# First attention layer and feed-forward layer in one block: the feed-forward layer's work is ordered behind single batches

## The reference, cut to what matters

```python
# first attention: one head, attention over the 128 columns (128x128 scores per batch)
x = x + layernorm(attn(layernorm(x)))
# feed-forward with ternary weights
def ternary_linear(x, w):                       # w_t: signs of w where |w| > 0.5 mean|w|, else 0
    rms = sqrt(sum(x * x)) / sqrt(d)
    return (x / (rms + 1e-8)) @ w_t.T
x = x + layernorm(ternary_linear(gelu(ternary_linear(layernorm(x), w_up)), w_down))   # 128 -> 512 -> 128
```

## Time and profile before

| | |
|---|---|
| time, median of 3 | 1156.36 us (1156.05 to 1159.06) |
| the profiled execution | 1163.83 us, span 1161.9 us |
| busy in the span: PE, DVE, ACT, POOL | 907.8, 597.1, 781.1, 360.5 us |
| first_attention | 0 to 90.2 us of the span |
| feed_forward | 90.7 to 191.2 us |
| all later blocks | 191.2 to 1161.9 us |

### The profile page before, as it was taken

The page is one execution under the profiler, slowest core; times in us unless marked ns, Lnnn a source line. Parts: engine busy times, 40 slices in busy tenths (PEclk is TensorE's granted clock), DMA queues, the critical chain, the costliest instruction groups (busy, mean ns, idle before and its releaser), DMA issues. The chain is left out here.

```text
span 1161.9 us, 19219 instructions
## 1 busy us (share of the span) xinstructions
PE 907.8 (78%) x6570; PEld 428.5 (37%) x6570; DVE 597.1 (51%) x2007; ACT 781.1 (67%) x1186; POOL 360.5 (31%) x332
## 2 busy tenths in 40 slices
PE   3754984765399999999989999998869878696650
PEld 3642763332021222222222222232357556365550
DVE  7387856888100444444443325342353236686557
ACT  1233342436499999999989999995565665675530
POOL 6312433445300000000000000222576477766743
PEclk8676986887699999999999999998959999898885
DMA  3000001235751212121111212245777655677741
GB/s 102 1 1 1 1 1 59 68 96 143 238 160 43 61 42 60 41 60 42 44 36 43 61 42 61 54 117 152 238 127 171 204 175 160 179 238 136 157 107 52
DMA packets 91259, 109.67 MB, mean 94 GB/s; under 512 B 11997, under 2 KB 62814, under 8 KB 91050
## 3 DMA queue, kind: packets, MB, share of 16 engines
q1 hardware_dynamic: 77128, 79.56, 23.1%
q0 software_dynamic: 12416, 27.80, 11.5%
q10 hardware_dynamic: 1634, 1.30, 0.4%
HBM read 68.90 MB, written 39.71 MB: 93 GB/s over the span
## 5 line engine op out<-in xcount | busy, mean ns | idle before, releaser
L1513 ACT ACTIVATE s_e<-s_ps 128x1024 f32<-128x1024 f32 x512 | 476.7, 1069 | 17.3 <-PE s_ps L1681 16.6
L1694 PE MATMUL s_acc<-s_e,s_v 128*32 128x512 f32 x2048 | 274.7, 609 | 0.7 <-ACT s_e L1513 0.7
L1135 POOL DMA_INDIRECT x_in<-x_tokens,rows_of x72 | 71.8, 997 | 464.8 <-DVE rows_of L1294 427.5
L1681 PE MATMUL s_ps<-s_q,s_k 51*128 51x512 bf16 x1024 | 180.6, 388 | 32.9 <-DMA s_k<-in_ones_row 13.3
L1681 PEld LDWEIGHTS s_ps<-s_q,s_k 51*128 51x128 bf16 x1024 | 41.2, 93 | 282.9 <-ACT s_e L1513 254.4
L2118 ACT ACTIVATE e_ht<-e_pn,ln_hid 128x288 f32<-128x288 f32 x192 | 85.9, 504 | 34.8 <-PE e_pn L2014 34.7
L2030 PE MATMUL e_py<-w,e_ht 128*96 128x128 f32 x768 | 108.7, 292 | 0.0
L2030 PEld LDWEIGHTS e_py<-w,e_ht 128*96 128x96 f32 x768 | 98.2, 179 | 0.0
L2000 PE MATMUL e_ph<-w,e_xt 128*32 128x512 f32 x576 | 79.0, 621 | 11.4 <-ACT e_hs L2085 6.8
L2014 PE MATMUL e_pn<-ident,e_hs 128*128 128x128 f32 x216 | 42.0, 314 | 44.8 <-ACT e_ht L2118 23.2
L1135 POOL DMA_INDIRECT e_ya<-y_rows,take x64 | 65.2, 1018 | 38.0 <-issue 29.9
(11 more groups left out here) (422 smaller groups left out, 1419.3 us busy)
## 6 DMA issues: line engine op xcount, KB each, us to landing
h_rows<-e_hs SPq DMA_DIRECT2D x54, 256.0 KB, 3.4
s_q<-parts_q SPq DMA_DIRECT2D x64, 96.0 KB
w<-in_w SPq DMA_DIRECT2D x1, 6144.0 KB, 20.7
s_k<-parts_k SPq DMA_DIRECT2D x62, 96.0 KB
h_rows<-x_res SPq DMA_DIRECT2D x18, 256.0 KB, 3.0
y_rows<-e_ys SPq DMA_DIRECT2D x24, 192.0 KB
s_k<-parts_k SPq DMA_DIRECT2D x62, 64.0 KB
parts_q<-b_parts SPq DMA_DIRECT2D x16, 192.0 KB, 2.7
```

What stands on the lines that cost most here:

```text
L1135: nc.gpsimd.indirect_dma_start(dst, None, rows, bass.IndirectOffsetOnAxis(ap=idx, axis=0), compute_op=op).then_inc(R["landed"][k % FLIGHT] ...
L1513: nc.scalar.activation(E[g % 4][:, 2 * pair:2 * pair + 2, :], pS[BUFFER["score", 2 * g + pair]][:].rearrange("p (a s) -> p a s", a=2), ACT ...
L1681: last = nc.tensor.matmul(pS[BUFFER["score", 2 * g + pair]][:, a * CH:(a + 1) * CH], K[c % 2][rows, pair, j * P:(j + 1) * P], Q[c % 2][row ...
L1694: last = nc.tensor.matmul(acc[hu % 2][32 * h:32 * h + 32, :], V4[c % 2][:, j, h, :], E[g % 4][:, h, :], start=j == 0, stop=j == TB - 1)
```

## The change

Both layers become one block, `first_layers`, without the meeting of all engines between them. The feed-forward part takes the PSUM buffers of the attention part, with waits on the reads of these buffers where they could still be in use, and has its own SBUF tiles and semaphores; the block has 59 semaphores. The steps of the feed-forward part have the prefix `f_` where the names met (`f_stats`, `f_std`, `f_normed`, `f_zt`, `f_scales`). The orders become:

```diff
 ACT
             std(0)
-            for b in range(B):
-                if b + 1 < B:
-                    std(b + 1)
-                if b < B - 1:
-                    normed(b)
+            std(1)
+            normed(0)
+            std(2)
+            normed(1)
+            f_std(0)
+            normed(2)
+            f_zt(0)
+            std(3)
+            f_std(1)
+            for k in range(NCH):
+                if k == 2:
+                    f_std(2)
+                    f_std(3)
+                if k + 1 < NCH:
+                    f_zt(k + 1)
...
 POOL
-            pool.wait_ge(ps, B)
+
+            for k in range(NCH):
+                pool.wait_ge(sq_done, FC * (k + 1))
...
 DVE
+            def f_stats(b):
+                tb = slice(b * TB, (b + 1) * TB)
+                if b < B - 1:
+                    v.wait_ge(ps, b + 2)
+                stats_of(nc, c, X[:, tb, :], f_st[:, tb, :], TB)
+                finish_stats(nc, c, f_st[:, tb, :], f_mean[:, tb], f_v128[:, tb], f_t1[:, tb],
+                             f_t2[:, tb]).then_inc(f_var_done, 1)
...
             for b in range(B):
+                if b == B - 1:
+                    f_stats(0)
+                    scales(b - 1)
                 add_output(b, 0)
                 if b + 1 < B:
                     m_copy(b + 1)
                 add_output(b, 1)
                 if b + 1 < B:
                     n_copy(b + 1)
+                if b == B - 1:
+                    f_normed(0)
                 v.wait_ge(o_read, 2 * b + 2)
                 stats(b, Y)
-                if b >= 1:
+                if 1 <= b < B - 1:
                     scales(b - 1)
+            f_stats(1)
             scales(B - 1)
...
             c.run(nc.vector.tensor_tensor(X[:, T - TB:, :], X[:, T - TB:, :], Y[:, T - TB:, :], ALU.add))
+            for k in range(NCH):
+                if k % 2 == 0 and k // 2 + 1 < B:
+                    f_normed(k // 2 + 1)
+                squares(k)
+                if k == 0:
+                    f_stats(2)
+                    f_stats(3)
+                if 2 <= k < NCH - 1:
+                    outputs(k - 2)
...
 PE (its order over chunks is as before; it follows output(3, 1) directly)
+                if k == 0:
+                    pe.wait_ge(signs_done, 1)
...
                 if k >= 2:
-                    pe.wait_ge(o_read, k - 1)
+                    pe.wait_ge(f_o_read, k - 1)
+                else:
+                    pe.wait_ge(o_read, 2 * (B - 1) + k + 1)
...
+                if k == 1:
+                    pe.wait_ge(b_read, B)
...
+        f_pT, pF, pD, pQ = pT, [pG, pR], pO, [pS, pM]
...
-            first_attention(nc, R, A)
-            feed_forward(nc, R, A)
+            first_layers(nc, R, A)
```

More of the change, by code:

```diff
@@ L230, in ternary @@
                     c.run(nc.vector.tensor_scalar(pk[:], w[:], thr[:, 2 + k:3 + k], None, ALU.is_lt))
-                    c.run(nc.vector.scalar_tensor_tensor(out[:], w[:], thr[:, k:k + 1], pk[:],
-                                                         ALU.is_gt, ALU.subtract))
+                    nc.vector.scalar_tensor_tensor(out[:], w[:], thr[:, k:k + 1], pk[:],
+                                                   ALU.is_gt, ALU.subtract).then_inc(signs_done, 1)
+                    v.wait_ge(signs_done, k + 1)
             def stats(b, src):
@@ new lines, in squares, with outputs @@
+            def squares(k):
+                for f in range(FC):
+                    v.wait_ge(h_done, FC * k + f + 1)
+                    if k >= 3 and f == 0:
+                        v.wait_ge(sum_mm, k - 2)
+                    nc.vector.tensor_tensor(SQ[:, k % 3, f, :], H[:, k % 2, f, :], H[:, k % 2, f, :],
+                                            ALU.mult).then_inc(sq_done, 1)
+            def outputs(k):
+                ts = slice(4 * k, 4 * k + 4)
+                v.wait_ge(down_mm, k + 1)
+                nc.vector.tensor_copy(f_O[:, ts, :], pD[k % 2][:].rearrange("p (t d) -> p t d", t=4)).then_inc(f_o_read, 1)
+                v.wait_ge(sum_mm, k + 1)
+                nc.vector.tensor_copy(ssq[:, ts], pQ[k % 2][:, 0:4]).then_inc(q_read, 1)
+                v.wait_ge(f_o_read, k + 1)
+                for t in range(4 * k, 4 * k + 4):
+                    c.mark(nc.vector.bn_stats(f_st[:, t, :], f_O[:, t, :]))
@@ L285, in _, with output_normed @@
+            def output_normed(b):
+                for t in range(b * TB, (b + 1) * TB):
+                    u = nc.vector.tensor_scalar(f_Z[:, t, :], f_O[:, t, :], mean2[:, t:t + 1], q1[:, t:t + 1],
+                                                ALU.subtract, ALU.mult)
+                return u
             v.wait_ge(ones_done, 5)
@@ L336, in _ @@
             c.run(nc.vector.tensor_tensor(X[:, T - TB:, :], X[:, T - TB:, :], Y[:, T - TB:, :], ALU.add))
+            for k in range(NCH):
[7 more added lines that the diff above has]
+                    outputs(k - 2)
+                if k == NCH - 2:
+                    outputs(NCH - 3)
+                    f_scales(0, PARTS[0])
+            output_normed(2).then_inc(u2_done, 1)
+            outputs(NCH - 2)
+            outputs(NCH - 1)
+            f_scales(1, PARTS[1])
+            c.run(output_normed(3))
+            c.run(nc.vector.tensor_tensor(X[:, T - TB:, :], X[:, T - TB:, :], f_Z[:, T - TB:, :], ALU.add))
         @block.tensor
@@ L622, in down @@
                 pe.wait_ge(h_done, FC * (k + 1))
+                if k == 0:
+                    pe.wait_ge(signs_done, 2)
                 if k >= 2:
[L624 removed]
+                    pe.wait_ge(f_o_read, k - 1)
+                else:
+                    pe.wait_ge(o_read, 2 * (B - 1) + k + 1)
                 for j in range(4):
```

264 lines of the change are left out of this document (93 added, 171 removed).

## The result

The changed kernel takes 1150.15 us (median of 20 runs, 1143.53 to 1154.17), the kernel before 1156.58 us beside it (20 runs). The two medians lie 6.43 us apart, a ratio of 0.9944; the ratio of the comparison is 0.9933, with a 95% interval of 0.9920 to 0.9946. The forecast of 1148.5 stood for a shift of 7.9 us, a ratio of 0.9932.

A forecast was written before the change was run, and what follows sets the result against it. Start-up waits on DVE's statistics, ACT's roots and the first Gelu, then PE bounds chunks 2 to 7. A gain of 9.9 us, partly given back at chunk 2, left 7.9: 1156.36 - 7.9 = 1148.5 us, range 1145.8 to 1152.5.

The forecast's parts named there:

- shift: How much earlier PE reaches transposes(4) than in the kernel before: 7.9 us, all carried to the end.
- Batch 0 and the two adds of POOL: End of attention: f_stats(0) at 77.82, f_normed(0) held by POOL's adds, first rows at 88.7, first Gelu at 95.8.
- Chunks 0 and 1: Feed-forward start: transposes(2) wait for DVE's rows until 100.65, transposes(3) over at 108.7, 9.9 us earlier than before.
- up(1) and the Gelus of chunk 1 follow as before: Chunk 1: old pattern kept, 9.9 us earlier; last Gelu over at 105.9.
- The hold on ACT at chunk 2: Deferred roots add two table loads, one covered; first Gelu of chunk 2 at 112.3, PE waits 2.15 us.
- The price of a load: ACT's table loads at chunk 2: 1.28 us each by the trace, without the skill's added drain of about 1.38 us.
- The sum: Whole kernel: 7.9 us less than the median of 1156.36, giving 1148.5 us; chance 0.42.
- The rival of the clock: PE's clock falls in the new gap at about 111: shift 5.7 us, time 1150.7; chance 0.25.
- The rival of DVE: DVE becomes the bound at transposes(4), 0.7 us in hand: shift 6 to 7; chance 0.13, shared with a longer gap.
- Only the seam: Between attention and feed-forward: DVE's chain decides, only the seam's 2.7 us is gained, time 1153.7; chance 0.09.
- The third block: Its head: POOL clears 59 semaphores in place of 20, 0 to 3.8 us of POOL, taken to cost nothing.

The follow-up runs named there:

- stats_beside: The changed kernel with f_normed(0) moved behind stats(3, Y), f_stats(1) and scales(3), so statistics run beside POOL's adds: 1193.11 us, 0.9903 of the kernel before.
- warm_pe: The changed kernel plus four extra 512-wide products in PE's pauses in chunks 0 and 1: 1194.05 us, 0.9883 of the kernel before.
- no_loads: The changed kernel with Identity for the roots of batches 2 and 3, so no table change at chunk 2: 1198.57 us, 0.9895 of the kernel before.
- roots_on_dve: The changed kernel with the roots of batches 2 and 3 computed on DVE in place of ACT: 1198.02 us, 0.9916 of the kernel before.
- early_only: The changed kernel, batch 0 still early, but statistics and roots of batches 2 and 3 again ahead of the first Gelu: 1205.64 us, 0.9949 of the kernel before.
- defer_only: The changed kernel with batch 0 treated behind the last add, batches 2 and 3 still deferred: 1201.62 us, 0.9935 of the kernel before.
- clears_59: The kernel before, with 39 more semaphore clearings on POOL at the head of the third block: 1156.51 us (one run).
- beside_again: The kernel of stats_beside, unchanged, run again on the third chip: 1146.12 us, 0.9892 of the kernel before.
- after: The changed kernel itself in its first measurement and profile: 1150.15 us, 0.9933 of the kernel before.
- after_again: The changed kernel, unchanged, run once more on another chip: 1194.90 us, 0.9891 of the kernel before.

## Why the prediction was right, step by step

- **Batch 0 and the two adds of POOL: right.** f_stats(0) at 78.44 (77.8, and 0.62 of offset), rows at 89.14 (88.7 and 0.62 would be 89.3), first Gelu at 96.16 (95.8 and 0.62 would be 96.4). What I didn't ask is what this order costs further on: stats_beside shows 3.5 to 3.9 us at transposes(4), of which 2.5 to 2.7 remain against warm_pe, where the clock is up in both.
- **Chunks 0 and 1: the mechanism right, one size off.** transposes(2) waited for DVE at 101.00 (100.65 and 0.62 would be 101.3). transposes(3) came at 110.18 instead of 109.3. The step "up(1) and the Gelus of chunk 1 follow as before" gave 8.05 us from transposes(2) to transposes(3), and they took 9.18; the clock was 0.50 for the first 3.2 us of them, and warm_pe, with 1.00, takes 7.60. The wait ahead of it was in my own numbers (products done at 94.2, Gelu at 95.8), and I had looked for a fall of the clock only at the gap near 111.
- **The hold on ACT at chunk 2: right in kind, its parts off by 0.6 to 1 us that cancel.** f_stats(2) ended at 107.42 and f_stats(3) at 109.82, as predicted without the offset, so 0.6 us ahead. The first load stands at 107.42 and not at 106.5 (105.9 and 0.62), because the last Gelu of chunk 1, late by the low clock, ends only at 107.41. It was hidden as I had said, since f_stats(3) came later still: in warm_pe it begins at 105.48, as the last Gelu ends, while the statistics for its root come at 107.1.

```profile
105.48 1.28 ACT L192 ACT_TABLE_LOAD   x1
...
107.11 0.30 ACT L192 ACTIVATE f_s<-f_s,consts 128x8 f32<-128x8 f32 x1 [0.34 <-DVE f_s L62]
```

  What I had wrong is what chunk 2's first Gelu waits for. I had it wait for f_stats(3) and the load behind it; in the trace ACT was free of the roots at 110.25, waited 0.57 us for PE's transposes(3), and the second load began behind the first product of up(2) (the bracket [0.34 <-PE]). So PE, late by the low clock, held ACT there. The first Gelu is at 113.04 where 112.9 was forecast, since DVE was 0.6 us ahead and PE 0.9 us late, and PE waited 1.19 us for it instead of 2.15. That these two cancel is luck.
- **The price of a load: by the row.** Behind all three loads the next ACTIVATE starts 0.01 to 0.02 us after the end (94.86 + 1.28 to 96.16, 111.75 + 1.28 to 113.04). The drain of 1.38 us that the Trainium skill adds in "ScalarE: Activation LUTs", section "What ACT_TABLE_LOAD costs", isn't to be seen in this trace. By it the uncovered load would have cost 2.66 us; both loads together cost 1.2 to 1.4 us at transposes(4) (no_loads).
- **The sum: right, with help from the two errors above.** 7.70 us at transposes(4), and 7.67 in the stretch, against 7.9; the ratio of 0.9933 is 7.75 us of 1156.36, the medians differ by 6.43. What stands at transposes(4) is carried to the third block; whether to the end, the time can't tell this closely, since single executions of one kernel lie up to 13 us apart.
- **The rival of the clock: it fell, but elsewhere.** In the gap at 113 it stayed at 1.00. warm_pe prices the fall at 97.4 at 1.1 to 1.2 us at transposes(4). So a part of this rival came true in a place where I hadn't looked; the shorter wait of PE in up(2), 1.19 us instead of 2.15, took most of it back against the forecast.
- **The rival of DVE: not here, but near.** 1.7 us in hand instead of 0.7: DVE's chain ran 0.8 us ahead of the forecast (with the offset), PE 0.2 behind it. roots_on_dve shows what happens without it.
- **"Only the seam": wrong, and well priced.** The seam alone is worth 2.8 us (2.7 forecast) at transposes(4), the rest is the two passes taken off the way to the first Gelu. What the change does for batch 0 brings nothing alone (early_only), and in this order nothing beside the deferral either (defer_only). I had given each part of the order its own saving; what counted was the way to the first Gelu, and behind it DVE's way to the rows of batch 1 and PE's clock.
- **The third block: right**, with one thing unforeseen, below.

What stays open: why the work from the expert layers on scatters by several microseconds from run to run, and whether the gain of stats_beside over the changed kernel, clear in both traces, is as large in the time. No run here settles either.

## What to carry to other kernels

When two stages meet, follow the chain to the first instruction of the engine that all others wait for, and move off it whatever isn't needed yet; starting the early batches sooner gains nothing while that chain stands, and is worth over 3 us once it is gone and the early work is not placed beside the other engine's adds (stats_beside against defer_only). On a pair of engines that hold each other up, order the work so that an operation that isn't held (here BATCH_NORM_STATS2, or one that reads PSUM) runs beside the other engine's long add: this was worth 2.5 to 2.7 us here, a third of the whole change, and another 1 us by the clock that it kept up, for no work saved. And where a trace of one execution must decide over a microsecond, measure from a point just ahead of the change to a point just behind it, not by the span, and look at what the clock did in between.

## What the runs showed of the hardware that was not expected

- A MEMSET on POOL, which reads nothing, holds DVE's TENSOR_SCALAR too. The eight of the third block take 2.66 us beside it (in the changed kernel and in clears_59) and 2.14 alone. The Trainium skill, "SBUF — State Buffer", section "Who interferes with whom", tells of a port pair that DVE and GpSimd share. The traces show DVE's operation held until POOL's ends (1.61 us beside one add, 4.27 and 5.26 us for eight beside the adds, and 2.14 for the same eight without).
- The two table loads of chunk 2 stand differently to the waits of the ACTIVATEs that need them. The one ahead of the roots begins as the last Gelu ends, though the statistics come 0.8 to 1.6 us later (defer_only, stats_beside, beside_again, warm_pe): idle time hides it. The one ahead of the Gelu, an ACTIVATE with three waits, begins about 0.1 us behind PE's first product wherever that product comes last (111.75 in the changed kernel, ACT free since 111.40). Why they differ, no run here settles.
- The attention part reaches POOL's add of batch 1 between 78.60 and 82.12 us in fourteen executions; on each of the three chips with four traces the spread is 2.9 to 3.2 us.
- PE's clock against the waits of PE: 1.00 was kept in waits of 0.58 (defer_only), 1.19 (after) and 1.79 us (warm_pe), and it fell behind those of 1.34 (roots_on_dve) and 2.35 us (after), while the earlier trace rows have one of 2.13 us that left it at 1.00. In after_again, the same kernel as after, it outlasted PE's wait of 2.04 us for the first Gelu and fell behind the next, of 2.21 us. So the length of the wait by itself doesn't tell; which other condition decides, no run here settles.
